# Attention: diagonal score parts of both pairs of heads share two PSUM banks, the bias fold goes in five pieces, and every engine gets a new order

## What is computed

```python
B, T, D = x.shape                       # 4, 2048, 256
H, HEAD_DIM = 16, 16
scores = einsum('bhqd,bhkd->bhqk', q, k) * HEAD_DIM ** -0.5
scores = where(k_pos > q_pos, -inf, scores)      # causal
m = max(scores, axis=-1)
p = softmax(scores - m)
out = einsum('bhqk,bhkd->bhqd', p, v)
```

## Time and profile before

| | |
|---|---|
| median of 3 runs | 4524.76 us (4506.0 to 4545.64) |
| the profiled execution | 4530.94 us, its span 4529.2 us |
| mean granted TensorE clock | 0.970 |
| attend(), from its first PE matmul to its last | 197.26 to about 1814 us of the span |
| PE, DVE, ACT, POOL busy over the span | 95%, 77%, 72%, 30% |

### The profile page before, as it was taken

How to read it: one execution, slowest core, us unless ns; L and a number is a source line. 1 busy time by engine, 2 the same in 40 slices (tenths; PEclk the granted TensorE clock), 3 DMA queues, 4 the chain that set the end, 5 groups by cost and what they waited for, 6 DMA issues and landing times. The chain is left out here.

```text
span 4529.2 us, 92469 instructions
## 1 busy us (share of the span) xinstructions
PE 4314.1 (95%) x31384; PEld 2883.4 (64%) x31384; DVE 3482.6 (77%) x8566; ACT 3277.8 (72%) x7769; POOL 1363.6 (30%) x1829
## 2 busy tenths in 40 slices
PE   7799999999999999599999999999999999999988
PEld 6634444444444443478787777777777777877767
DVE  7688889999988995477777777776777777777745
ACT  2267777777877778387878778786887878787853
POOL 3112222222222222333333333333333333333303
PEclk9789899999989999799999999999999999999989
DMA  8823344332333330200000000010100000000007
GB/s 288 284 42 60 60 99 77 82 55 55 68 69 66 73 75 18 81 25 15 20 24 20 24 20 25 20 44 23 68 25 20 25 20 24 15 20 24 20 18 293
DMA packets 177908, 270.05 MB, mean 60 GB/s; under 512 B 79025, under 2 KB 105265, under 8 KB 176689
## 3 DMA queue, kind: packets, MB, share of 16 engines
q1 hardware_dynamic: 173344, 260.27, 21.2%
q10 hardware_dynamic: 4112, 4.00, 0.4%
HBM read 158.25 MB, written 105.38 MB: 58 GB/s over the span
## 5 line engine op out<-in xcount | busy, mean ns | idle before, releaser
L743 ACT ACTIVATE a_pt<-a_ring 128x512 f32<-128x512 f32 (+3 forms) x2560 | 1172.4, 545 | 358.4 <-PE a_ring L860 348.0
L793 DVE TENSOR_REDUCE a_mx<-a_ring 128x1 f32<-128x512 f32 (+2 forms) x1904 | 1158.7, 667 | 101.7 <-PE a_ring L874 75.2
L1157 POOL TENSOR_TENSOR l_rn<-l_ssm,l_half 128x8 f32<-128x8 f32 x256 | 431.0, 1684 | 1132.2 <-DVE l_ssm L1415 1132.1
L898 PE MATMUL a_ot<-a_pt,a_vt 128*32 128x512 f32 (+3 forms) x5120 | 613.8, 554 | 2.1 <-POOL a_pt L683 1.0
L874 PE MATMUL a_ring<-s_ks,s_qs 48*128 48x512 f32 (+3 forms) x2560 | 555.8, 430 | 47.6 <-PEq L136 18.8
L860 PE MATMUL a_ring<-s_qs,s_ks 49*128 49x512 f32 (+3 forms) x2560 | 562.6, 444 | 27.2 <-DVE a_mx L789 19.1
L1246 ACT ACTIVATE l_pr<-l_pr,l_negm 128x256 f32<-128x256 f32 (+1 forms) x1024 | 505.9, 504 | 2.8 <-DVE l_negm L1467 2.4
L860 PEld LDWEIGHTS a_ring<-s_qs,s_ks 49*128 49x128 f32 x2560 | 250.7, 188 | 369.2 <-ACT a_pt L743 178.6
L1262 ACT ACTIVATE l_pr<-l_pr,l_rden 128x256 f32<-128x256 f32 (+1 forms) x1024 | 457.1, 507 | 24.8 <-DVE l_rden L1475 21.9
L874 PEld LDWEIGHTS a_ring<-s_ks,s_qs 48*128 48x128 f32 x2560 | 259.4, 193 | 332.7 <-ACT a_pt L743 225.8
L1164 POOL TENSOR_TENSOR l_work<-l_work,e_rot 128x512 f32<-128x512 f32 x256 | 345.7, 1350 | 306.7 <-DVE l_work L1423 306.7
(11 more groups left out here) (167 smaller groups left out, 8945.2 us busy)
## 6 DMA issues: line engine op xcount, KB each, us to landing
qk_d<-p_parts SPq DMA_DIRECT2D x16, 2048.0 KB, 10.4
s_qs<-qk_d SPq DMA_DIRECT2D x180, 128.0 KB, 6.5
s_ks<-qk_d SPq DMA_DIRECT2D x180, 128.0 KB, 9.7
e_rot<-rot_s SPq DMA_DIRECT2D x32, 512.0 KB, 4.0
x_d<-l_dx SPq DMA_DIRECT2D x32, 512.0 KB, 2.7
e_xt<-x_d SPq DMA_DIRECT2D x24, 513.0 KB, 5.0
p_x_in<-x SPq DMA_DIRECT2D x16, 512.0 KB, 9.0
x_d<-p_xt SPq DMA_DIRECT2D x16, 512.0 KB, 5.2
```

Of the source, the lines that this page charges most:

```text
L743: act.activation(pt[:, (g * STEPS + s) % NPT, 2 * piece + f, q0:CHUNK], bank("step", g, k, f)[:, q0:CHUNK], ACT.Exp).then_inc(exp_done.sem, 1)
L793: dve.tensor_reduce(mx[:, pr, f:f + 1, t, kc], ring[:, banks[f], 0:w], AX.X, ALU.max)\
L898: mm = pe.matmul(ot[j * VW:(j + 1) * VW, q0:CHUNK], vt[:, v, kt, j], pt[:, (G * STEPS + s) % NPT, j, q0:CHUNK], start=kt == 0, stop=kt == ...
L1157: pool.tensor_tensor(out=rn[:, a * HEADS:(a + 1) * HEADS], in0=ssm[:, a * HEADS:(a + 1) * HEADS], in1=half[:, 0:HEADS], op=ALU.pow).then_i ...
```

## The change

- The two narrowest diagonal parts (256 and 128 columns) of a step are made for both pairs at once: the matmuls of both pairs go into the same two banks side by side, and ACT takes one exp over both pairs for each bank. Slots per group: 80 before, 72 after. The same for the two narrowest units (t = 0 and 1 on the diagonal): 80 units before, 72 after; DVE reduces both pairs and, where the banks are neighbours, all four heads in one instruction. POOL masks four heads in one instruction there. The matmuls themselves stay.
- The fold has no bank and no event of its own. Its 11 matmuls go in five pieces (3, 2, 2, 2, 2) into spare columns of five narrow units, and DVE adds each piece to b1.
- PE's order (tensor_order()) and the orders of SP, POOL, ACT and DVE are new. The first step of chunk 2 is step 20 now, of chunk 3 step 42. row_out of chunks 1 and 2 comes right at the start of an iteration on PE. In SP's order, row_out of chunk 2 stands behind load.
- In prepare(), ACT waits for the constants before it issues its 16 small DMAs.

```diff
+            act.wait_ge(consts, 96)
             act.wait_ge(ones_set, 1)
...
+        both = tuple(range(NPAIR))
+        units = [(c, prs, t, kc) for c in range(CPB) for prs in ((0,), (1,)) for t in range(TPC)
+                 for kc in range(c + 1) if kc < c or t >= TPC // 2]
+        for c in range(CPB):
+            for t in range(TPC // 2):
+                where = [n for n, u in enumerate(units) if u[0] == c and u[1] == (0,) and (u[2], u[3]) > (t, c - 1)]
+                units.insert(where[0], (c, both, t, c))
+        slots = [(s, pieces) for s, (c, kt) in enumerate(steps)
+                 for pieces in (((0,), (1,)) if kt < TPC * c + TPC // 2 else (both,))]
...
+        fold_at = {units.index((0, both, 0, 0)): range(0, 3), units.index((0, (0,), 2, 0)): range(3, 5),
+                   units.index((0, (1,), 2, 0)): range(5, 7), units.index((1, both, 0, 1)): range(7, 9),
+                   units.index((1, (0,), 2, 1)): range(9, MB)}
...
         def tensor_order(do):
+            do("step", 0); do("unit", 43); do("weigh", -3); do("step", 1); do("unit", 44); do("weigh", -2)
+            do("row_out", 1); do("row_out", 2); do("unit", 45); do("step", 2); do("unit", 46); do("weigh", -1)
+            do("step", 3); do("unit", 47); do("step", 4); do("weigh", 0); do("step", 5); do("unit", 48)
+            do("step", 6); do("unit", 49); do("step", 7); do("unit", 50); do("weigh", 1); do("step", 8)
+            do("unit", 51); do("step", 9); do("weigh", 2); do("out", -1); do("unit", 52); do("step", 10)
+            do("weigh", 3); do("unit", 53); do("step", 11); do("unit", 54); do("weigh", 4); do("unit", 55)
+            do("step", 12); do("unit", 56); do("weigh", 5); do("step", 13); do("unit", 57); do("step", 14)
+            do("unit", 58); do("weigh", 6); do("step", 15); do("unit", 59); do("step", 16); do("weigh", 7)
+            do("step", 17); do("unit", 60); do("step", 18); do("out", 0); do("step", 19); do("unit", 61)
+            do("step", 20); do("unit", 62); do("weigh", 8); do("step", 21); do("unit", 63); do("step", 22)
...
+            do("unit", 80); do("row_out", 3); do("step", 39); do("unit", 81); do("row_out", 4); do("step", 40)
+            do("unit", 82); do("weigh", 18); do("step", 41); do("unit", 83); do("step", 42); do("unit", 84)
...
         @block.sync
...
             def around(do):
-                do("row_out", 1); do("out", -3); do("row_out", 2); do("out", -2); do("out", -1); do("load", 1)
-                do("row_out", 3); do("out", 0); do("item_out", -1); do("row_out", 4); do("keep", 0)
-                do("item_in", 1)
+                do("row_out", 1); do("out", -1); do("load", 1); do("row_out", 2); do("out", 0)
+                do("item_out", -1); do("out", 1); do("row_out", 3); do("out", 2); do("row_out", 4)
+                do("keep", 0); do("item_in", 1)
...
         @block.scalar
...
+                    if pieces == both:
+                        out_ = pt[:, (g * STEPS + s) % NPT, f:GH:2, q0:CHUNK]
+                        in_ = bank("step", g, k, f)[:, 0:NPAIR * (CHUNK - q0)].rearrange("p (r n) -> p r n", r=NPAIR)
...
             def around(do):
+                do("step", 0); do("step", 1); do("row_copy", 1); do("row_copy", 2); do("step", 2)
+                do("raw_out", -1)
...
         @block.vector
...
+                if prs == both and banks[1] == banks[0] + 1:
+                    pieces = ring[:, banks[0]:banks[1] + 1, 0:NPAIR * w].rearrange("p f (r n) -> p f r n", r=NPAIR)
+                    dve.tensor_reduce(mx[:, :, :, t, kc].rearrange("p r f -> p f r"), pieces, AX.X, ALU.max)\
+                       .then_inc(mm_used.sem, 2)
```

More of the change, by code:

```diff
@@ L396, in attend @@
         STEPS = sum(TPC * (c + 1) for c in range(CPB))
-        UNITS = sum(TPC * NPAIR * (c + 1) for c in range(CPB))
-        SLOTS = NPAIR * STEPS
+        UNITS = sum(TPC * NPAIR * (c + 1) - TPC // 2 for c in range(CPB))
+        SLOTS = NPAIR * STEPS - TPC // 2 * CPB
         NG = BATCH * NGROUP
@@ L497, in tensor_order @@
         def tensor_order(do):
[L498 to L522, removed]
@@ new lines, in tensor_order @@
+            do("step", 25); do("unit", 66); do("weigh", 11); do("unit", 67); do("step", 26); do("unit", 68)
+            do("weigh", 12); do("step", 27); do("unit", 69); do("step", 28); do("weigh", 13); do("unit", 70)
+            do("step", 29); do("unit", 71); do("weigh", 14); do("step", 30); do("unit", 72); do("unit", 73)
+            do("step", 31); do("weigh", 15); do("step", 32); do("unit", 74); do("unit", 75); do("step", 33)
+            do("weigh", 16); do("step", 34); do("unit", 76); do("out", 1); do("unit", 77); do("step", 35)
@@ new lines, in tensor_order @@
+            do("unit", 89); do("step", 47); do("weigh", 23); do("unit", 90); do("step", 48); do("unit", 91)
+            do("step", 49); do("weigh", 24); do("unit", 92); do("step", 50); do("unit", 93); do("weigh", 25)
+            do("step", 51); do("out", 2); do("unit", 94); do("step", 52); do("unit", 95); do("step", 53)
+            do("unit", 96); do("step", 54); do("unit", 97); do("step", 55); do("unit", 98); do("weigh", 26)
+            do("step", 56); do("unit", 99); do("step", 57); do("weigh", 27); do("unit", 100); do("step", 58)
@@ L534, in attend @@
+            do("step", 69); do("unit", 113); do("step", 70); do("weigh", 36); do("step", 71); do("unit", 114)
         held = [None] * NB
@@ L719, in around @@
             def around(do):
-                for n in range(0, 35):
+                for n in range(0, 43):
+                    do("step", n)
+                do("split", 0)
+                for n in range(43, 49):
                     do("step", n)
                 do("widen", 1)
[L723 to L726, removed]
+                for n in range(49, 72):
                     do("step", n)
@@ L915, in out @@
                 mm.then_inc(otr_done.sem, 1)
-            def fold(G, _):
-                l, kind, k = items[G]
-                if kind != "w1":
-                    return
-                pe.wait_ge(small_in, 16 * 5)
-                pe.wait_ge(raw_in.sem, raw_in.at(G))
-                wait_for_banks(pe, "fold", G, 0)
-                for m in range(MB):
-                    mm = pe.matmul(bank("fold", G, 0)[:, m:m + 1], w_raws[:, G % 2, m * P:(m + 1) * P], lnb[:, l, k:k + 1],
-                                   start=True, stop=True)
-                mm.then_inc(folded.sem, 1)
-            program(dict(step=step, unit=unit, weigh=weigh, row_out=row_out, out=out, fold=fold), tensor_order)
+            program(dict(step=step, unit=unit, weigh=weigh, row_out=row_out, out=out), tensor_order)
 def layers(nc, x_d, split_d, kept, lasting, wmask_d, ident_d, first_loads):
```

194 lines of the change are left out of this document (105 added, 89 removed).

## The result

The changed kernel takes 4704.66 us (median of 4 runs, 4704.15 to 4711.34), the one before 4520.88 us (median of 4, its three and one more beside the new one). The ratio is 1.041, interval 1.038 to 1.043: 184 us slower. The forecast was 4753 us, range 4630 to 4825.

The account below looks back on a forecast made before the run. PE and DVE, almost in lockstep through a shared ring of seven banks, were taken to bound the kernel; 4529.2 - 30 - 25 + 225 + 48 + 5 + 5 = 4757 us span, forecast 4753 us, range 4630 to 4825.

Parts of the forecast that it names:

- Shapes, -30: Merged narrow steps and units: 2.0 us gained in each of 15 iterations, between the savings of DVE (1.3) and ACT (2.7).
- The fold, -25: Four iterations lose 35.2 us to the fold; 4 x 2.6 us of matmuls stay as cost, the rest is gained.
- The wait, +225: PE's first step of chunk 2 waits 16.1 us for row_out 2, issued behind the load, in each of iterations 1 to 14.
- T: The time of PE's out -1 in an iteration, 665.47 us in the earlier trace.
- The row of 11.8 us: Profile row: a load of 512 KB issued behind 3 MB took 11.8 us; basis for choosing the 16.1 us wait.
- rival A: Row_out 2 is not held up by the load: wait of 4.2 us, no clock cost, 4539 us; chance 0.13.
- The clock, +48: After each of 14 long waits PE starts at half clock: 3.4 us lost each, bounds 0 and 6.8.
- Rival B: The lower clock after PE's waits costs its upper bound, 48 us more: 4801 us; chance 0.17.
- Iteration 0, +5: PE's wait for row_out 2 in iteration 0, where the load starts some 7 us earlier: 5 us, bounds 0 and 9.
- row_out 3, +5: Three units ahead of step 42 take 3.4 us, the row's chain 3.8: 0.3 us in each of 15 iterations.
- Constants and mask, nothing: ACT's wait for constants in prepare() and POOL's mask over four heads were both priced at nothing.
- Rival C: Freed bank turns let DVE run without waits, 9.2 us per iteration: 4635 us with the long wait, 4421 with 4.2; chance 0.08.

Follow-up runs that it names:

- the row first: The changed kernel with one edit: SP issues row_out 2 ahead of out -1 and the load; 4463.53 us, ratio 0.987 to the kernel before.
- the kernel with separate exps: Against the row first: ACT and DVE read each pair's part of the shared banks in separate instructions; 4468.56 us, ratio 0.989 to the kernel before.

## Why the prediction was right, and where its sizes were off

The sum was 4757 us of span and the span is 4702.5. Term by term, in the order of the prediction:

- **Shapes, -30.** Right in size, by luck: 2.3 us an iteration, 35 together (47 by the runs without the fold). Wrong in its reason. I took a value between the savings of ACT and DVE; undone, these savings cost 5 us or nothing by the medians. What is left to gain by is that 16 turns of the ring fall away, in an order made for it; the banks shared are worth 162 us there and the new orders lose 115. Such a gain can't be read from busy times.
- **The fold, -25.** Too large: 1 to 8 us by the runs without it, 17 by the iterations of the earlier trace rows against those of the row first. I took all but 10 of the 35.2 for gained; the block cost no more than 21 and the pieces cost 13.5 to 19.5. Beside the block the clock was down in all four iterations. It is so beside the pieces in two of four of the changed kernel, and in none of four of the kernel with separate exps. The window of the changed kernel around one of them is

```profile
640.00:660.00 20.00, 19.86 (x150) 8.29 (x144) 15.22 (x27) 12.22 (x25) 10.60 (x15) 0.81 0.00 1
```

- **The wait, +225.** The mechanism is right, its place too: 203.5 us for the 14, 14.5 where 16.1 was put. PE arrives at T + 13.3 (12.7) and goes on at T + 26.8 (28.8). The row of 11.8 us in the earlier trace rows was the right neighbour, and rival A, with 4.2, is out. Its premise that 4.2 us are too short to count on a lower clock is out as well: in the kernel with the row in the middle of the load, waits of 1.31 to 3.54 us have it behind them. Two of its steps were wrong without harm to it. The row is not held because it is on the same queue: on ACT's it takes as long. And its issue does not take 1.05 us but 11.12.
- **The clock, +48.** Too large. By spans, 4702.5 - 4472.7 = 229.8 lie between the changed kernel and the row first, 206.2 of them waits: 23.6 are left, 1.7 for each of 14 (2.5 by medians), where 3.4 was put and up to 6.8 possible. After these 14 waits the lower level lasts 5.8 us on average, which is 2.9 lost, near my 3.4; about a us of it does not show in the total, and where it is made up was not tried. Rival B is out here; the 4.7 of the old kernel with the row last lies beyond my value, and the lower level lasts 12.2 to 15.2 us there. The Trainium skill (Trainium Kernel Development and Optimization, Performance Expectations) calls matmul busy time a bad metric for how close a kernel is to the limit. The trace agrees, for a reason of its own: PE is busy for 5.81 us of 5.81 in the window after the wait, at half its clock.
- **Iteration 0, +5, and row_out 3, +5.** 2.7, and no wait at all.
- **Constants and mask, nothing.** No difference to be told for the first; the masks over four heads take 0.634 us, and nothing waits for them at length.
- **Rival C.** The wait does not feed back into faster iterations: without it they are 93.5 us, so the whole change is worth 2.3 us an iteration and not 9.2.

Measured, the terms are -35 - 17 + 204 + 24 + 3 = +179; the span grew by 173. The prediction is 48 us above the median, for the most part wait and clock. (Its chance of slower by over 1% adds up to 0.83 by its own terms, not 0.84.)

## What to carry to other kernels

Before you move a small transfer past a large load, read how long the load takes to land, not how long it takes to issue: whatever was issued late in it arrived late here, on both queues tried. Ask it of every row that the engine setting the end waits for, and place that row ahead of the load. And take an order written for a ring together with its number of turns: the new orders without the saved turns lost 115 us, more than the 47 that both together gained.

After any wait of the engine that sets the time, read the clock until it is full again, in more than one place: the length of the wait does not tell how long that takes.

## What the runs showed of the hardware

- The issue that follows a 512 KB transfer behind 3 MB of others is held on SP's queue: 11.12 us for the row, 13.50 for the store of an output. With v at the head of the load the row's issues take 1.04 and nothing is held. An engine that computes would stand still as long if its own issue were held like that, which was not tried. The rows do not say what fills up.
- The row, two transfers of 4 KB, took 9.2 us from SP's queue and 9.4 from ACT's in the middle of the same load, and 14.1 from ACT's at its end.
- How long the granted clock stays at 0.50 after a wait of PE does not follow from the length of the wait. A wait of 3.54 us had 16.6 us of it behind it, with PE busy all the time, and one of 13.56 had 5.8. Waits of 1.31 to 3.54 us cost 1.5 to 2.7 us each beyond the wait, those of the changed kernel 1.7 to 2.5, and those of the old order (7.6 to 13.3 us) 4.7, with 12.2 to 15.2 us at 0.50 behind each.
